# A decoder layer on one core: the state-space step input dt*u made by GpSimd in SBUF, and its PSUM bank used as a fourth gate bank

## The reference

```python
dt = softplus(einsum('blr,dr->bld', dt_in, W_dt) + dt_bias)
dA = exp(dt[..., None] * A)                        # 16 states for each of 512 channels
dBu = dt[..., None] * Bm[:, :, None, :] * u[..., None]
h = da * h + dbu                                   # scan over 512 tokens
y = einsum('bdn,bn->bd', h, c)
...
r = sigmoid(xr + hr); z = sigmoid(xz + hz); n = tanh(xn + r * hn)   # three rounds
slots = (1.0 - z) * n + z * h
```

## Time and profile before

| what | value |
|---|---|
| time before, median of 2 runs | 1582.78 us (1582.43 to 1583.13) |
| profiled execution, its own time | 1578.58 us |
| its span, first to last instruction | 1576.8 us |
| mean granted TensorE clock | 0.921 of full speed |
| DVE busy in the span | 1320.2 us (84%) |
| PE busy in the span | 1320.8 us (84%) |
| ACT busy in the span | 993.4 us (63%) |
| POOL busy in the span | 873.1 us (55%) |

### The profile page before, as it was taken

One profiled execution on the slowest core, in us unless ns is written; L12 is line 12 of the kernel. 1 busy time (PEld: TensorE's weight loads), 2 busy tenths in 40 slices (PEclk: granted clock), 3 DMA queues, 4 the chain that ended last, 5 costly groups with the idle time before them and its releaser, 6 DMA issues. The chain is left out here.

```text
span 1576.8 us, 16668 instructions
## 1 busy us (share of the span) xinstructions
PE 1320.8 (84%) x5624; PEld 802.8 (51%) x5624; DVE 1320.2 (84%) x1463; ACT 993.4 (63%) x1581; POOL 873.1 (55%) x470
## 2 busy tenths in 40 slices
PE   5665886597899888897898978998898978998997
PEld 3344544364465545564465644564455644555454
DVE  3999689886898899988998799988899899984545
ACT  5543566457677477747776487756776587654632
POOL 0666257754676467763776457763676558761000
PEclk8775899797999989999999989998999989998999
DMA  7633343316233163315432063324433163320000
GB/s 247 227 132 120 128 169 119 108 54 230 94 120 107 58 227 120 121 67 188 144 110 106 28 244 131 120 80 145 164 110 116 40 230 134 108 84 9 7 7 27
DMA packets 64293, 188.50 MB, mean 120 GB/s; under 512 B 6257, under 2 KB 22001, under 8 KB 64241
## 3 DMA queue, kind: packets, MB, share of 16 engines
q1 hardware_dynamic: 64240, 187.84, 34.3%
HBM read 183.10 MB, written 4.72 MB: 119 GB/s over the span
## 5 line engine op out<-in xcount | busy, mean ns | idle before, releaser
L517 POOL TENSOR_TENSOR reg_a<-reg_a,cb 128x1024 f32<-128x1024 f32 (+1 forms) x256 | 605.2, 2373 | 308.6 <-DVE reg_a L1442 308.4
L1442 DVE TENSOR_TENSOR_SCAN reg_a<-reg_a,pb 128x1024 f32<-128x1024 f32 x256 | 585.0, 2285 | 18.2 <-ACT reg_a L1173 1.6
L1173 ACT ACTIVATE reg_a<-dt,neg_a 128x511 f32<-128x511 f32 x512 | 334.8, 711 | 61.7 <-DVE reg_a L1442 61.2
L806 PE MATMUL py<-ident,reg_a 128*128 128x128 f32 x1984 | 278.7, 290 | 65.9 <-POOL reg_a L517 65.2
L1433 DVE TENSOR_TENSOR pb<-bb,pb 128x1024 f32<-128x1024 f32 x256 | 314.0, 1227 | 18.7 <-DMA bb<-bc_rows 1.6
L806 PEld LDWEIGHTS py<-ident,reg_a 128*128 128x128 f32 x1984 | 244.7, 150 | 148.9 <-POOL reg_a L517 81.4
L659 PE MATMUL px<-hT,whh 128*128 128x512 f32 x252 | 120.4, 609 | 0.0
L771 PE MATMUL pc<-x2T,w_fc 128*128 128x512 f32 x192 | 93.8, 611 | 15.4 <-ACT reg_m L1096 8.0
L779 PE MATMUL pc<-w_pr,reg_m 128*128 128x256 f32 x384 | 90.2, 383 | 3.4 <-ACT reg_m L1098 3.4
L740 PE MATMUL pc<-xnT,w_in 128*128 128x512 f32 x128 | 76.7, 731 | 13.5 <-DVE sz L1345 12.4
L1080 ACT ACTIVATE xs<-px,half_b 128x512 f32<-128x512 f32 x63 | 41.0, 685 | 68.2 <-PE px L664 36.4
(11 more groups left out here) (277 smaller groups left out, 2378.7 us busy)
## 6 DMA issues: line engine op xcount, KB each, us to landing
bb<-bc_rows SPq DMA_DIRECT2D x256, 512.0 KB, 3.6
cb<-bc_rows SPq DMA_DIRECT2D x64, 512.0 KB, 6.5
xin<-x_in SPq DMA_DIRECT2D x8, 512.0 KB, 3.4
xs<-x_in SPq DMA_DIRECT2D x8, 512.0 KB, 3.3
x_out<-reg_m SPq DMA_DIRECT2D x5, 512.0 KB, 3.0
...
```

Source lines behind the costliest of these rows:

```text
L517: pool.tensor_tensor(h[:, g % HR, 0:n], h[:, g % HR, 0:n], cb[:, 2 * q:2 * q + n], ALU.mult).then_inc(s["hc_done"], 1)
L806: mm = pe.matmul(py[:, cols_], h[:, g % HR, j, cols_], ident[:], is_transpose=True, start=(q == 0 and j == 0 and i2 == 0), stop=(q == PAIR ...
L1173: ins = act.activation(d_a[:, g % DR, j, 1:], dt[:, c, 1:], ACT.Exp, scale=neg_a[:, c * NS + n + j:c * NS + n + j + 1])
L1442: dve.tensor_tensor_scan(h2[:, g % HR], d_a2[:, g % DR], pb[:, 1:3, :].rearrange("p a t -> p (a t)"), 0.0, ALU.mult, ALU.add).then_inc(s[" ...
```

## The change

- POOL makes the step inputs of chunks 1 to 3, right after their `dt`, into `sp[:, c]`, an SBUF tensor that was free from then on; DVE makes the first one there too (`first_input`). `step_input` between the chunks is gone.
- `mul` reads the step input from `sp` in SBUF, where it read the PSUM bank `pb[:, 0]`. Its waits stay the same.
- `pb[:, 0]` becomes a bank of gate 2. Gate 3 has `px[:, 0]` to itself and waits for `renorm`; the candidates take the banks of gates 0 and 1 and wait for one tanh less each.
- The table of fillers has new places for many steps.

```diff
-        g_banks = (px[:, 0, :], px[:, 1, :], pb[:, 3, :])
-        gate_bank = (g_banks[1], g_banks[2], g_banks[0], g_banks[1])
-        cand_bank = (g_banks[2], g_banks[0])
+        gate_bank = (px[:, 1, :], pb[:, 3, :], pb[:, 0, :], px[:, 0, :])
+        cand_bank = (px[:, 1, :], pb[:, 3, :])
...
                 pool.tensor_tensor(dt[:, c], dt[:, c], sp[:, c], ALU.add).then_inc(s["dt_ready"], 1)
+                if c:
+                    pool.wait_ge(s["dt_ready"], c + 1)
+                    pool.wait_ge(s["dtu_ready"], c)
+                    pool.tensor_tensor(sp[:, c], dt[:, c], u2[:, c], ALU.mult).then_inc(s["dtu_ready"], 1)
...
                     if j == 1 and k == 0 and mamba:
                         pe.wait_ge(s["sp_abs"], DT)
-                    elif j == 2:
+                    elif j == 2 and k == 0 and mamba:
+                        pe.wait_ge(s["sp_abs"], 1)
+                    elif j == 3:
                         pe.wait_ge(s["an_done"], k + 1)
-                    elif j == 3:
-                        pe.wait_ge(s["trz_ready"], 4 * k + 1)
...
-                    pe.wait_ge(s["trz_ready"], 4 * k + 2 + j)
+                    pe.wait_ge(s["trz_ready"], 4 * k + 1 + j)
...
-                def step_input(c):
+                def first_input():
 
-                    dve.wait_ge(s["dt_ready"], c + 1)
-                    dve.tensor_tensor(pb[:, 0, :], dt[:, c], u2[:, c], ALU.mult).then_inc(s["dtu_ready"], 1)
+                    dve.wait_ge(s["dt_ready"], 1)
+                    dve.tensor_tensor(sp[:, 0], dt[:, 0], u2[:, 0], ALU.mult).then_inc(s["dtu_ready"], 1)
...
-                    dve.tensor_tensor(pb[:, 1:3, :], bb[:, g % HB], pb[:, 0:1, :].to_broadcast([P, 2, L]),
+                    dve.tensor_tensor(pb[:, 1:3, :], bb[:, g % HB], sp[:, c:c + 1, :].to_broadcast([P, 2, L]),
                                       ALU.mult).then_inc(s["mul_done"], 1)
...
                     if mamba:
-                        if g < GROUPS - PAIRS and g % PAIRS == PAIRS - 1:
-                            step_input(g // PAIRS + 1)
                         if g + 1 < GROUPS:
                             mul(g + 1)
```

The new places of DVE's and POOL's fillers, and of PE's at the start and the end of a pass (ACT's table and the rest of PE's change in the same way, by a place or two):

```diff
+        at("pe", ("start", ("load",)), (1, ("ctx", 1), ("ctx", 2), ("ctx", 3), ("norm", 0), ("gate_h", 0, 0), ("x2t", 0), ("x2t", 1)),
...
+                      (30, ("u", 0), ("u", 1), ("final", 0)), (31, ("u", 2), ("u", 3)), (33, ("outp", 0)),
+                      (34, ("outr",), ("xp", 0), ("outp", 1), ("outp", 2), ("outp", 3), ("xp", 1), ("xp", 2), ("xp", 3)))
...
+        at("dve", ("start", ("spike", 0), ("ctx", 0), ("spike", 1), ("ctx_norm",)), ("head", ("spike", 2), ("spike", 3), ("spike", 4)),
+                      (("mid", 0), ("spike", 5)), (("mid", 2), ("score", 0)), (("mid", 3), ("soft", 0)), (3, ("soft2", 0), ("recol", 0)),
+                      (("mid", 4), ("zed", 0)), (4, ("out_stats",)), (("mid", 5), ("renorm", 0)), (("mid", 6), ("zed", 1)), (6, ("out_shift",)),
+                      (7, ("hold", 0)), (("mid", 8), ("zed", 2)), (("mid", 9), ("zed", 3)), (("mid", 12), ("score", 1)), (12, ("next_stats",)),
+                      (("mid", 13), ("soft", 1), ("next_shift",)), (13, ("soft2", 1)), (("mid", 14), ("recol", 1)), (14, ("renorm", 1)),
+                      (17, ("hold", 1)), (("mid", 22), ("score", 2)), (("mid", 24), ("soft", 2), ("soft2", 2)), (24, ("recol", 2)),
+                      (("mid", 25), ("renorm", 2)), (25, ("down", 1, 1)), (("mid", 28), ("hold", 2)), (28, ("down", 1, 3)), (31, ("conv", 0, 0)),
+                      (("mid", 32), ("conv", 0, 1), ("conv", 0, 2), ("conv", 2, 0)), (33, ("final", 0), ("final", 1)),
+                      ("end", ("conv", 2, 1), ("conv", 2, 2)))
-        at("pool", ("start", ("ctx", 0), ("spike", 0)), (1, ("dt", 1)), (2, ("dt", 2)), (3, ("out_stats",)), (5, ("dt", 3)),
-                      (8, ("keep", 0), ("cand", 0)), (10, ("next_stats",)), (16, ("keep", 1)), (18, ("cand", 1)), (27, ("keep", 2)), (28, ("cand", 2)),
-                      (32, ("final", 1)))
+        at("pool", ("start", ("ctx", 0), ("spike", 0)), (3, ("dt", 1), ("out_stats",)), (6, ("dt", 2), ("dt", 3)), (7, ("keep", 0)), (8, ("cand", 0)),
+                      (12, ("next_stats",)), (17, ("keep", 1)), (18, ("cand", 1)), (27, ("keep", 2)), (28, ("cand", 2)), (34, ("final", 1)))
```

More of the change, by code:

```diff
@@ L301, in at @@
                 plan[(engine, position)] = steps
-        at("pe", ("start", ("load",), ("ctx", 1), ("ctx", 2)), (1, ("ctx", 3), ("norm", 0), ("gate_h", 0, 0), ("x2t", 0), ("x2t", 1)),
-                      (3, ("colsum", 0), ("zed", 0), ("gate_h", 0, 1), ("spread", 0)), (4, ("zed", 1)),
+        at("pe", ("start", ("load",)), (1, ("ctx", 1), ("ctx", 2), ("ctx", 3), ("norm", 0), ("gate_h", 0, 0), ("x2t", 0), ("x2t", 1)),
+                      (3, ("colsum", 0), ("zed", 0)), (4, ("zed", 1), ("gate_h", 0, 1), ("spread", 0)),
@@ L305, in decoder_layer @@
                       (5, ("gate_x", 0, 0), ("gate_x", 0, 1), ("gate_h", 0, 2), ("gate_h", 0, 3), ("gate_x", 0, 2), ("gate_x", 0, 3)),
[L306 removed]
+                      (6, ("cand_h", 0, 0), ("cand_h", 0, 1), ("zed", 2), ("cand_x", 0, 0), ("cand_x", 0, 1)), (8, ("zed", 3)), (9, ("up", 0, 0)),
                       (10, ("norm", 1), ("up", 0, 1)), (11, ("up", 0, 2)), (12, ("up", 0, 3)), (13, ("gate_h", 1, 0)),
[L308 removed]
@@ L313, in decoder_layer @@
[L313 to L331, removed]
-                      (13, ("soft", 1)), (("mid", 14), ("soft2", 1), ("recol", 1)), (("mid", 15), ("renorm", 1)), (("mid", 18), ("hold", 1)),
-                      (("mid", 23), ("score", 2)), (24, ("soft", 2)), (("mid", 25), ("soft2", 2), ("recol", 2), ("renorm", 2)), (25, ("down", 1, 1)),
-                      (("mid", 28), ("hold", 2)), (28, ("down", 1, 3)), (("mid", 31), ("conv", 0, 0), ("conv", 0, 1)),
-                      (("mid", 33), ("conv", 0, 2), ("conv", 2, 0), ("conv", 2, 1)), (33, ("final", 0), ("final", 1)), (("mid", 34), ("conv", 2, 2)))
@@ L336, in decoder_layer @@
-        at("pool", ("start", ("ctx", 0), ("spike", 0)), (1, ("dt", 1)), (2, ("dt", 2)), (3, ("out_stats",)), (5, ("dt", 3)),
-                      (8, ("keep", 0), ("cand", 0)), (10, ("next_stats",)), (16, ("keep", 1)), (18, ("cand", 1)), (27, ("keep", 2)), (28, ("cand", 2)),
-                      (32, ("final", 1)))
+                      (14, ("down", 0, 0), ("colsum", 1), ("gate_h", 1, 1)),
+                      (15, ("spread", 1), ("down", 0, 1), ("gate_x", 1, 0), ("gate_x", 1, 1), ("gate_h", 1, 2), ("gate_h", 1, 3), ("gate_x", 1, 2)),
@@ new lines, in decoder_layer @@
+                      (16, ("gate_x", 1, 3), ("cand_h", 1, 0), ("cand_h", 1, 1)),
+                      (17, ("down", 0, 2), ("down", 0, 3), ("cand_x", 1, 0), ("cand_x", 1, 1)), (18, ("up", 1, 0)),
+                      (20, ("turn",), ("up", 1, 1), ("norm", 2), ("gate_h", 2, 0)), (22, ("up", 1, 2)), (23, ("up", 1, 3)),
+                      (24, ("down", 1, 0), ("down", 1, 1), ("colsum", 2), ("gate_h", 2, 1), ("spread", 2)),
+                      (25, ("gate_x", 2, 0), ("gate_x", 2, 1), ("gate_h", 2, 2), ("gate_h", 2, 3), ("gate_x", 2, 2)), (26, ("gate_x", 2, 3)),
```

18 lines of the change are left out of this document (14 added, 4 removed).

## The result

The changed kernel takes 1921.1 us (2 runs, 1919.0 to 1923.3) against 1582.8: ratio 1.213, 95% interval 1.210 to 1.216. The forecast was 1870, the range 1670 to 1995. The profiled execution took 1918.99 us, its span 1917.2. The lines of the code have moved: the multiply is now L1438, the scan L1447, POOL's product L522, its sum for `dt` L503, its new step input L507, DVE's first step input L1428.

A forecast was written before the change was run, and what follows sets the result against it. DVE's groups were taken as the bound, with multiplies held behind POOL's products. Stretches add 60+2x31+5x33 = 287 us, step inputs' 40 us gain included, to 1578.6: 1866, stated as 1870 us, range 1670 to 1995.

The forecast's parts named there:

- POOL is first by 0.02 to 0.03, the multiply waits out its product and ends 1.09 later: Quiet group on DVE: the multiply is held behind POOL's product, so a group of 3.71 us becomes 5.91.
- 3 us for waits on PE and ACT: Later passes on DVE: remaining waits for PE and ACT add 3 us to a stretch of 183.7.
- the relief: Later passes: where POOL is not ready at the scan's end, multiplies meet less than a full product, saving 18 us.
- The fillers behind the multiplies: Later passes on DVE: fillers the new places put between multiply and scan are not hidden and add 13.2 us.
- The granted clock: PE in later passes: at an estimated clock of 0.85 its work takes 155 us, still inside 184.
- Step inputs off DVE, -40: DVE between scan and next multiply: 24 of 32 step inputs leave, gaining 40 us over eight passes.
- Step inputs onto POOL, 1.27 each: POOL: 24 added products at 1.27 us, 30 us in all, hidden in POOL's idle time.
- The multiply alone, 0: DVE's multiply with two SBUF operands, away from POOL, costs nearly the same, 1.22 against 1.23 us: 0 in the sum.
- A fourth gate bank, 0: Gates and candidates wait for fewer tanhs: between 0 and -2 us, hidden by longer groups, so 0.
- New places, 0, and 7 either way: Between passes, steps move by a slot or two: -1 to +1 us each of 7 times, 0 in sum.
- No conflict: Rival: a row of 512 read twice does not collide with POOL, so multiplies are not held: 1541 us, chance 0.06.
- Multiply first: Rival: in quiet groups the multiply starts before POOL's product, which then runs under the next scan: 1675 us, chance 0.12.

The follow-up runs named there:

- e1: Kernel before, with only DVE's step inputs written to SBUF tensor sp and read there by the multiply: 1884.2 us, ratio 1.190 to the kernel before.
- e3: Changed kernel with the multiply's wait for the scan put ahead of those for bb and the step input: 1669.3 us, ratio 1.054 to the kernel before.
- e5: Changed kernel with DVE's last down sum moved from place 28 to 29, behind scan 29: 1885.0 us, ratio 1.191 to the kernel before.
- e2: Kernel before with only the changed kernel's new table of places: 1558.0 us, ratio 0.984 to the kernel before.
- e10: Kernel before with DVE's step inputs of chunks 1 to 3 put ahead of their slot's fillers: 1558.9 us, ratio 0.985.
- e8: Kernel before with the new places, and DVE's last down sum moved from place 28 to 29: 1547.9 us, ratio 0.978.

## Why the prediction was right

*What bounds a quiet group.* The step "POOL is first by 0.02 to 0.03, the multiply waits out its product and ends 1.09 later" was right to the hundredth: 5.91 forecast, 5.90 measured, with the same three gaps. e1 shows that the operand alone does it, e3 that the order of start decides.

*The passes.* First pass 186 forecast, 186.2 measured. Second 181.5 (150.5 and 31), measured 181.0. The six passes with a feed-forward part were forecast to grow by 33 us (the last by 31) and grew by 39.8 to 42.6; the fifth took 192.2 where 183.7 was forecast. The term that was mis-sized is "3 us for waits on PE and ACT". In the fifth pass DVE waited 9.7 us at three lines: 7.5 at L1358 and 2.2 at two others. I took the waits of the kernel before as covered by longer groups and did not look for new ones in the new places, though the two tables in the diff show it: DVE takes `down` ahead of scan 29, PE makes it in place 29. e5 puts DVE's step behind the scan, and the pass takes 185.4. The six passes together miss by 52 us: 287 forecast, 338.7 measured between the first and the last scans.

The rest of the fifth pass was right to 2 us, in part by luck. A multiply held for a whole product ends 3.52 us behind its scan (1005.92 against 1002.40); added up over the pass, the others end 13 to 14 us earlier than that, where the relief was put at 18. Most of the difference is at place 18, with 3.5 for 5.9. The fillers behind the multiplies cost 11 us, where 13.2 was forecast. The two misses nearly cancel.

*The granted clock.* The forecast spread a lower clock over the whole pass, where it is hidden. It did fall to 0.87 as a mean there, but what cost time is one place: PE idle for 3.66 us, then at half pace, with DVE waiting for it. In the fifth pass PE's queue, from the first candidate sum to the end of the `down`, takes 9.58 us at 0.51. In e2, where PE was not idle ahead of it, the same queue runs at 1.00:

```profile
850.97:856.10 5.13, 5.13 (x23) 3.19 (x23) 0.40 (x1) 1.39 (x3) 5.05 (x5) 1.00 0.00 0
```

So it is in all six passes of e2 and of e3, 5.12 us each time; in the changed kernel the six take 8.35 to 9.68, 25 us more in all, and DVE waits for their end. Of the 43.8 us of the wait at L1358 the lower clock therefore makes 25. The 19 that are left are less than e2's 29.0, because the held multiply in front covers more of PE's queue (DVE is busy for 2.15 us of it, for 0.40 in e2), and near e3's 21.0. That a lower clock is hidden is the other step of the prediction that failed here: it is worth about half of the 52 us.

*Step inputs off DVE, -40.* DVE keeps eight, 5.5 us, so 40 left it. But 24 of these 40 were holds that order alone removes (e10).

*Step inputs onto POOL, 1.27 each.* They take 1.56 in the mean, 37.3 us for 30; they too are held now and then. As forecast, POOL is not the bound.

*The multiply alone, 0.* e3 shows it without a hold at 1.23 with both operands in SBUF, the value of the earlier trace rows with one in PSUM. The estimate from the Trainium skill's page "VectorE: DVE Perf Modes" (errata section), 65 ns less for each, is not borne out.

*A fourth gate bank, 0.* DVE's wait for the second candidate, 15.0 us at L1388, is no longer among the waits of the changed kernel. But the bank is not shown to be the cause: with the old banks the wait is 1.0 us in e2, by the new places, and 3.5 us in e1, by the operand. By itself the bank was not tried, because it is free only when the operand has left it.

*New places, 0, and 7 either way.* In the kernel before they give 25 us (e2), and 35 with the late `down` put right (e8), so the term was too small there. In the changed kernel they bring the wait at L1358: it takes 37 us more than e1, which has the operand alone, and e5's one step takes 36 of these back.

*The sum by rows of DVE.* Multiplies 711.2 - 314.0 = +397; step inputs -40; L1358's wait 43.8 - 12.5 = +31; the waits of the earlier trace rows 16.5 to 7.8 and 15.0 to 0, and two smaller ones 11.5 to 0.6 (L1345, now L1350) and 6.2 to 0 (L1475, now L1478), together -41. Added up, they give 347, against 340 us by which the span grew; the 7 over are small terms that were not followed.

*The rivals.* "No conflict" fell at the first group: an operand of one row read twice collides as any other. "Multiply first" did not come about by itself, but e3 brings it about, and takes 1669.3 us where the rival was priced at 1675; its fifth stretch, 163.8 us, is 13.0 longer than before, as priced. So the chance of it hung on 0.02 us of lead, as written. The Trainium skill says in "SBUF — State Buffer", section "Who interferes with whom", that the port pair shared by the two engines is an exclusive lock and that issue order decides who blocks; e3 agrees, since moving the multiply's start by 0.07 us exchanges 3.42 and 2.35 (multiply, POOL) for 1.23 and 3.40.
